# A fused attention and expert-layer kernel: the router loaded in rows on ScalarE's queue, and the hand-off from routing to the first token tiles reordered

## The chip, the cores and the metric

The kernel runs on one core of a Trainium2 chip. The metric is the device time of one execution in microseconds (us), as the median of several runs. Before the change it is 2000.14 us (three runs, 1999.53 to 2000.66).

## The reference, cut to what matters

```python
xn = layernorm(x)                       # x: 4 x 1024 x 1024, 4096 tokens in all
k, v = xn @ Wk.T + bk, xn @ Wv.T + bv
kv_sum = cumsum((elu(k) + 1) * v, axis=tokens of one sequence)
s = ((elu(xn @ Wq.T + bq) + 1) * kv_sum * SCALE) @ Wo.T + bo
logits = xn @ router_w.T                # 8 experts, the best 2 of each token
...                                     # at most 256 slots per expert, in token order
h = gelu(buf @ w1.T + b1) @ w2.T + b2   # buf: the tokens kept in their slots
g = silu(scatter(h * probs))
out = x + s * g
```

A token that no expert keeps has g = 0, so that its row of the output is x. The kernel therefore computes q, s and the expert layer only for the tokens that are kept, gathered into 2048 slots; only k, v and their running sum run over all tokens up to the last kept one.

## The kernel before, in words

**Numbers.** A product of float32 matrices is made from float16 halves: HI is the rounded value, LO the rest, and three products (HI HI, HI LO, LO HI) are added in PSUM. Making such a pair is two steps: a copy on ScalarE (`high_...`) and a scale-and-subtract on VectorE (`low_...`).

**Stage 1, the scores.** The transposed input x_t comes in 8 blocks of 512 tokens, each in two halves of 1 MB (the first half of block 0 in two quarters), on SyncE's DMA queue, behind the router's weights (line 502). TensorE starts with 11 matmuls on zeros (line 1921). Then `scores_by_expert` (line 1893) multiplies float32 x by `rw_f`, the router's weights with a ninth column of ones, 8 chunks of 128 features for each block; ScalarE copies the 9 x 512 result out (line 922), and `scores_by_token` (line 1906) turns it into rows of tokens. VectorE corrects for the mean, takes the top 2 (lines 1331 to 1345) and, behind each block, the LO halves of some of the 16 chunks of Wk and Wv (`WKV_BEHIND`: how many chunks ScalarE and VectorE split behind which block; chunks 12 to 15 are behind the last).

**Stage 2, the hand-off.** When the last block is routed, VectorE works through a chain of small operations: places of all choices within their experts (lines 1365 to 1377), which tokens are kept (1380, 1381), ranks of kept tokens (1391 to 1395), the selection matrix of tile 0 (`kept_columns`, 1399), starts of tiles and counts of loops (1405 to 1424, the signal `tables_ready`). TensorE gives it two pairs of matmuls on the way (1968/1969 and 1975/1976) and fills the time with projections of tile 0 (`project_chunks`, line 1955): half n of four is 8 chunks of 3 matmuls of 128 x 128 by 128 x 512, n = 0, 1 being k and n = 2, 3 being v, into banks 0 to 3. Then it selects: `KEPT` (line 1993) for tile 0's own kept columns, and `select_x` (line 1984) in four steps s = 0 to 3 for tile 1, each transposing half of one of HI and LO and picking the kept columns. `read_selected` (lines 492 to 497) copies both results out of PSUM, on ScalarE for s = 0, 2 and on VectorE for s = 1, 3.

**Stage 3, the token tiles.** A tile t of 128 tokens is projected while VectorE and ScalarE turn k into phi(k), multiply by v and split the product; `sum_kv` (line 2006, 16 matmuls) of the *previous* tile makes the running sums of the kept columns, and `sums` (VectorE, 1451 and 1457) adds the carry and puts them into a window that SyncE stores. Tile 0 has no previous tile: `kv_hl` and the matrix `upto[1]` are set to zero (1382, 1421) and the same code runs on zeros. ScalarE stores blocks of zeros behind the last slot (line 954). All tiles from 2 on run in a loop whose count is read from `loops_i`.

**Stage 4** is the expert layer, q and Wo, in products that are combined from sums of weights; GpSimd makes these sums (lines 784 to 812) from the moment when tile 1's k v product is split, and stores them in DRAM. It fills the time from about 500 us to the end.

**What sets the order.** Every engine has one list of instructions, written by hand, which it runs in order; semaphores tie the lists together. `stage_done` counts TensorE's transposes and selections, `stage_act` and `stage_dve` the reads of them, `wkv_ready` the chunks split, `select_ready`, `tables_ready`, `ranks_ready` and `kept_ready` the steps of the routing chain.

Of the kernel before, what the change touches and what calls it, by code (L numbers as in the profile page):

```python
# [10 lines left out]
ALU = mybir.AluOpType  # L11
# [76 lines left out]
def apart(eng):  # L88

    eng.nop(nofuse=True)  # L90


def build(nc, x, x_t, w_kv, router, w_up, w_down, b_k, b_v, b_q, b_o, b_1, b_2, out):
# [13 lines left out]
    with ExitStack() as ctx:  # L107
# [163 lines left out]
        nothing = part(16, 1)[:, 0:BLOCK // 2]  # L271
        rw_chunks = table(N4, "p (e o) -> p e o", e=EXPERTS, o=1)
# [217 lines left out]
        WKV_BEHIND = ((), (), (0,), (1, 2), (3, 4), (5, 6, 7, 8), (9, 10, 11), (12, 13, 14, 15))  # L490
# [10 lines left out]
        def _(sp):  # L501
            sp.dma_start(rw_f[:, :, 0:EXPERTS], router).then_inc(router_loaded, 16)


# [35 lines left out]
            sp.wait_ge(tables_ready, 1)  # L540
            pairs = sp.value_load(loops_i[0:1, 0:1], min_val=2, max_val=TILES // 2)
            sp.wait_ge(tables_ready, 2)
# [196 lines left out]
        def _(pool):  # L739
# [34 lines left out]

            pool.wait_ge(wkv_ready, 2 * CH)
            pool.wait_ge(tables_ready, 1)
# [130 lines left out]
        def _(act):  # L907

            def high_wkv(q):
                act.wait_ge(wkv_loaded[q % WL], 16 * (q // WL + 1))  # L910
                nc.scalar.activation(wkv[:, q, HI, :], kv_stage[q], ACT.Copy, scale=WS).then_inc(wkv_hi, 1)
# [5 lines left out]
            for b, weights in enumerate(WKV_BEHIND):  # L917
# [33 lines left out]
            with act.Fori(0, tails) as n:  # L951
                at = nc.s_assert_within(kept + n * P, 0, SLOTS)
                apart(act)
                act.dma_start(win_dram[:, :, ds(at, P)], zeros).then_inc(tail_stored, 16)
# [11 lines left out]
            def tile(t, u, first=False, second=False):  # L966
# [10 lines left out]
                at = act.value_load(start_i[0:1, ds(t + 2, 1)], min_val=0, max_val=SLOTS)  # L977
                for s in range(4) if second else (0, 2):
# [26 lines left out]

            tile(0, 0, first=True)
            tile(1, 1, second=True)
            with act.Fori(1, pairs) as g:
                for u in range(2):
                    tile(2 * g + u, u)  # L1010
# [250 lines left out]
        def _(dve):  # L1261
# [3 lines left out]
            for i, (s, n) in enumerate(((logits_read, 2), (proj_read, 4), (win_stored, 32), (tail_stored, 16),  # L1265
                         (kv_ready, 2), (stage_dve, 2))):
                nc.vector.memset(scratch[i], 0.0).then_inc(s, n)
            dve.wait_ge(router_loaded, 16)
            nc.vector.tensor_reduce(rw_chunks[:, :, :], rw_f[:, :, 0:EXPERTS].rearrange("p c e -> p e c"),
# [151 lines left out]
            nc.vector.memset(upto[1][:, :], 0.0)  # L1421
            kept_columns(1, 1)
# [18 lines left out]
            pairs = dve.value_load(loops_i[0:1, 0:1], min_val=2, max_val=TILES // 2)  # L1441
# [18 lines left out]
            def tile(t, u, g, first=False, second=False):  # L1460
# [78 lines left out]
            tile(1, 1, 0, second=True)  # L1539
            with dve.Fori(1, pairs) as g:  # L1540
# [347 lines left out]
        def _(pe):  # L1888
# [31 lines left out]
            for _ in range(11):  # L1920
                mm(out_bank(2), zeros[:, 0:P], zeros, start=True, stop=True)
            pe.wait_ge(router_loaded, 16)
# [7 lines left out]
            pe.wait_ge(zeros_ready, 2)  # L1930
            mm(bank[3][:, 0:EXPERTS], ones_f, rw_chunks[:, :, 0], start=True, stop=True).then_inc(sums_w_done, 1)
            second_half(0, 1, range(CH // 2, CH)).then_inc(scores_done, 1)
            pe.wait_ge(zeros_ready, 3)
# [15 lines left out]
            scores_by_token(1, TOKEN_BLOCKS - 1)  # L1949
# [13 lines left out]
            project_chunks(0, 0, range(CH)).then_inc(proj_done, 1)  # L1963
# [8 lines left out]
            pe.wait_ge(wkv_ready, 2 * CH)  # L1972
# [4 lines left out]
            project_chunks(0, 2, range(CH // 2, CH)).then_inc(proj_done, 1)  # L1977
# [13 lines left out]
            for h in (HI, LO):  # L1991
# [3 lines left out]
                ins.then_inc(stage_done, 1)  # L1995
# [72 lines left out]
            pe.wait_ge(tables_ready, 1)  # L2068
# [194 lines left out]
```

## Time and profile before

| | |
|---|---|
| median of three runs | 2000.14 us |
| the profiled execution, its own time | 2000.25 us |
| its span in the trace | 1998.0 us |
| TensorE busy | 1970.9 us, 99% |
| VectorE, ScalarE, GpSimd busy | 69%, 35%, 25% |
| mean granted clock of TensorE | 0.997 |

The profile lists, for each engine, groups of instructions by their line in the kernel and their start in us from the start of the span. PE is TensorE (PEld its loads of weights), DVE VectorE, ACT ScalarE, POOL GpSimd, SP SyncE; SPq, ACTq are the parts of these engines that issue DMAs. In a row of the timeline the bracket is the time for which the engine stood idle before the group, and the instruction whose end released it.

### The profile page before, as it was taken

The page shows a single profiled execution, that of the slowest core. Times are in us where ns is not written, and L with a number is a line of the kernel's source. Part 1 is how long each engine was busy: PE and PEld are TensorE (multiplying, and loading weights), DVE is VectorE, ACT ScalarE, POOL GpSimd, SP SyncE. Part 2 cuts the span into 40 slices and gives each one's busy share as a digit, 9 for nine tenths or more (in the row PEclk, how much of TensorE's full clock was granted, in tenths as well). Part 3 has the DMA queues.
Part 4 walks back from the last instruction along what each step waited for, and adds up shares of the span by engine and source line. Part 5 has one row for each costly group of instructions (what it writes and reads, how often), then busy time and mean ns, then how long its engine had stood idle before and what let it go on. Part 6 is the DMA issues. An engine that isn't in the chain of part 4 may idle for free.

```text
span 1998.0 us, 27184 instructions
## 1 busy us (share of the span) xinstructions
PE 1970.9 (99%) x9393; PEld 902.9 (45%) x9393; DVE 1378.4 (69%) x2101; ACT 707.4 (35%) x1112; POOL 504.6 (25%) x640
## 2 busy tenths in 40 slices
PE   9999999999999999999999999999999999999996
PEld 2455554455444444444444444444444444444442
DVE  4887878887877777776777797564455565456656
ACT  1432223222754344344335443522212322322322
POOL 0048888888312321321310010210000000000002
PEclk9999999999999999999999999999999999999998
DMA  9546667667999988978777879673333233335535
GB/s 388 203 141 221 228 228 236 227 212 205 304 331 286 254 243 268 281 235 279 251 263 236 293 257 324 201 222 101 102 104 101 90 114 102 111 106 159 183 114 129
DMA packets 182203, 416.26 MB, mean 208 GB/s; under 512 B 18592, under 2 KB 71376, under 8 KB 179664
## 3 DMA queue, kind: packets, MB, share of 16 engines
q1 hardware_dynamic: 138736, 284.26, 43.4%
q0 software_dynamic: 34896, 121.71, 20.0%
q10 hardware_dynamic: 8464, 8.92, 1.5%
q8 instruction: 60, 0.98, 0.2%
q14 instruction: 47, 0.39, 0.1%
HBM read 268.51 MB, written 163.10 MB: 216 GB/s over the span
## 4 chain that ended last, share of the span: by engine, by line
PE 92%; DVE 3%; DMA 2%; issue 1%; ACT 1%; SPq 0%; DVEq 0%; POOL 0%; ACTq 0%; POOLq 0%
PE pair L2145 36%; PE pair L2116 34%; PE pair L1955 16%; PE pair L1893 3%; PE pair L1984 1%; DMA arena<-up_sums 1%; PE pair L2006 1%; DMA spare<-up_sums 0%; PE pair L1906 0%; DMA arena<-x_t 0%; DVE arena L1548 0%; PE pair L2085 0%; DVE arena L1321 0%; DVE root L1300 0%; DVE arena L1315 0%
## 5 line engine op out<-in xcount | busy, mean ns | idle before, releaser
L2145 PE MATMUL pair<-arena 128*128 128x512 f16 x3360 | 730.2, 379 | 1.1 <-DVE arena L1694 0.5
L2116 PE MATMUL pair<-xnT,arena 128*128 128x512 f16 x2400 | 525.4, 379 | 2.1 <-ACT xnT L1044 1.9
L2145 PEld LDWEIGHTS pair<-arena 128*128 128x128 f16 x3360 | 327.8, 98 | 400.2 <-issue 7.2
L1686 DVE SCALAR_TENSOR_TENSOR arena<-pair,arena 128x1024 f32<-128x1024 f32 x234 | 286.0, 1223 | 150.7 <-PE pair L2145 149.8
L1955 PE MATMUL pair<-arena 128*128 128x512 f16 x1728 | 382.9, 379 | 1.7 <-DVE xnT L497 1.0
L1118 ACT ACTIVATE arena<-arena 128x512 f16<-128x512 f32 x280 | 171.4, 626 | 554.8 <-PE pair L2145 500.0
L2116 PEld LDWEIGHTS pair<-xnT,arena 128*128 128x128 f16 x2400 | 234.4, 98 | 286.6 <-ACT xnT L1044 3.4
L1955 PEld LDWEIGHTS pair<-arena 128*128 128x128 f16 x1728 | 168.6, 98 | 194.1 <-issue 1.9
L2116 PE MATMUL pair<-xnT 128*128 128x512 f16 x960 | 213.7, 379 | 0.0
L1661 DVE SCALAR_TENSOR_TENSOR arena<-arena 128x512 f16<-128x512 f32 x280 | 189.3, 688 | 16.4 <-ACT arena L1118 15.7
L839 POOL DMA_DIRECT2D s_dram<-arena x8 | 6.2, 776 | 596.4 <-DVE arena L1686 596.4
L1044 ACT ACTIVATE xnT<-pair 128x512 f32<-128x512 f32 x120 | 71.2, 594 | 220.2 <-PE pair L2116 220.1
L2116 PEld LDWEIGHTS pair<-xnT 128*128 128x128 f16 x960 | 93.9, 98 | 113.3
L858 POOL DMA_INDIRECT meta_dram<-meta,slot_i x32 | 33.5, 1048 | 367.0 <-PE pair L2145 304.7
L1567 DVE SCALAR_TENSOR_TENSOR arena<-arena 128x1024 f16<-128x1024 f32 x70 | 85.5, 1223 | 27.6 <-ACT arena L1037 27.1
L1105 ACT ACTIVATE arena<-arena,b_c 128x512 f32<-128x512 f32 x96 | 69.2, 721 | 74.7 <-DVE arena L1597 39.1
L972 ACT ACTIVATE arena<-arena 128x512 f32<-128x512 f32 x36 | 22.7, 629 | 162.4 <-DVE arena L1465 162.4
L1604 DVE TENSOR_TENSOR arena<-xnT,pair 128x512 f32<-128x512 f32 x40 | 27.4, 686 | 74.2 <-PE pair L2116 74.0
L1561 DVE SCALAR_TENSOR_TENSOR arena<-arena 128x512 f16<-128x512 f32 x82 | 59.0, 720 | 21.5 <-ACT arena L1026 20.0
L1037 ACT ACTIVATE arena<-arena 128x1024 f16<-128x1024 f32 x70 | 72.8, 1043 | 0.0
L1608 DVE TENSOR_TENSOR arena<-xnT,pair 128x512 f32<-128x512 f32 x40 | 27.5, 687 | 62.7 <-ACT xnT L1044 62.7
L1597 DVE TENSOR_TENSOR arena<-xnT,pair 128x512 f32<-128x512 f32 x40 | 27.4, 685 | 54.4 <-PE pair L2116 53.9
(217 smaller groups left out, 1817.5 us busy)
## 6 DMA issues: line engine op xcount, KB each, us to landing
down_dram<-arena SPq DMA_DIRECT2D x70, 512.0 KB, 7.0
arena<-down_dram SPq DMA_DIRECT2D x70, 512.0 KB, 3.3
up_dram<-arena SPq DMA_DIRECT2D x90, 256.0 KB, 6.0
arena<-up_dram SPq DMA_DIRECT2D x90, 256.0 KB, 2.6
arena<-down_sums SPq DMA_DIRECT2D x40, 512.0 KB, 6.1
arena<-w_up POOLq DMA_DIRECT2D x36, 512.0 KB
up_sums<-arena POOLq DMA_DIRECT2D x36, 512.0 KB, 3.8
arena<-up_sums SPq DMA_DIRECT2D x66, 256.0 KB, 6.1
```

What stands on the lines that cost most here:

```text
L1037: nc.scalar.activation(down_ring[:, j, :, HI, :], down_stage[d % DS].rearrange("p (c n) -> p c n", c=2), ACT.Copy, scale=WM).then_inc(down ...
L1044: nc.scalar.activation(dst, in_rows(src), ACT.Copy).then_inc(copy_ready, 1)
L1105: nc.scalar.activation(g_block(name), src, ACT.Gelu, bias=b1_c[:, col:col + 1], scale=INV_XM)\
L1118: nc.scalar.activation(g_ops[:, A_NAMES.index(name), k % 2, HI, :], g_block(name), ACT.Copy, scale=CS if is_attention(n) else HS).then_inc ...
L1561: nc.vector.scalar_tensor_tensor(up_ring(j)[:, LO, :], up_stage[a % US], WM, up_ring(j)[:, HI, :], ALU.mult, ALU.subtract).then_inc(up_w[j ...
L1567: nc.vector.scalar_tensor_tensor(down_ring[:, j, :, LO, :], down_stage[d % DS].rearrange("p (c n) -> p c n", c=2), WM, down_ring[:, j, :, ...
L1661: nc.vector.scalar_tensor_tensor(to[:, LO, :], g_block(name), CS if is_attention(k // 2) else HS, to[:, HI, :], ALU.mult, ALU.subtract).th ...
L1686: ins = nc.vector.scalar_tensor_tensor(to, src, scale, to, ALU.mult, ALU.add)
L1893: ins = mm(scores(u), rw_f[:, c, :], xt_in[u][:, c, :], start=(c == 0), stop=(c == CH - 1))
L1955: ins = mm(out_bank(n), xT[u][:, a, c, :], wkv[:, (n // 2) * CH + c, b, e], start=(c == 0 and i == 0), stop=(c == CH - 1 and i == 2), skip ...
L2116: ins = mm(out_to, w[:, a, c * P:(c + 1) * P], x_in_op[:, b, c, :], start=(first and i == 0), stop=(i == 11), skip_group_check=True)
L2145: ins = mm(down_banks(j, t // 2)[:, (t % 2) * BLOCK:(t % 2 + 1) * BLOCK], g_ops[:, A_NAMES.index(DOWN_A[j]), c, a, t * P:(t + 1) * P], dow ...
```

## The change

The router's weights are loaded contiguously into a scratch table `rw_in`, from ScalarE's queue, and VectorE copies them into `rw_f`; SyncE's first DMA is now x_t. TensorE runs 8 matmuls on zeros, not 11. The three matmuls of the first chunk of projection 0 stand ahead of the last `scores_by_token`. VectorE splits chunks 14 and 15 behind `kept_ready`, not ahead of the places; both selection matrices are made one after the other; two subtractions for the softmax move behind them and raise `tables_ready` by one, on which ScalarE now reads `KEPT`. For tile 0, `sum_kv` and `sums` are gone; GpSimd sets `kv_hl` and window 0 to zero. TensorE's `select_x` steps for tile 1 and the projection chunks between them are dealt out anew, and ScalarE reads step 0 ahead of its stores of zeros.

```diff
-        WKV_BEHIND = ((), (), (0,), (1, 2), (3, 4), (5, 6, 7, 8), (9, 10, 11), (12, 13, 14, 15))
+        WKV_BEHIND = ((), (), (0,), (1, 2), (3, 4), (5, 6, 7, 8), (9, 10, 11), (12, 13))
+        WKV_LAST = (14, 15)
 @block.sync
-            sp.dma_start(rw_f[:, :, 0:EXPERTS], router).then_inc(router_loaded, 16)
 @block.gpsimd
+            pool.wait_ge(scores_done, TOKEN_BLOCKS)
+            nc.gpsimd.memset(kv_hl[:, :, :], 0.0).then_inc(kvlo_ready, 2)
+            pool.wait_ge(wkv_ready, 12)
+            nc.gpsimd.memset(window[0], 0.0).then_inc(win_ready, 1)
 @block.scalar
+            act.dma_start(rw_in, router).then_inc(router_loaded, 16)
...
+            for q in WKV_LAST:
+                high_wkv(q)
+            act.wait_ge(wkv_ready, SOON)
             act.wait_ge(tables_ready, 1)
-            act.wait_ge(wkv_ready, SOON)
             for h in (HI, LO):
                 act.wait_ge(stage_done, 3 + h)
                 ins = copy(xnT[:, h, :, 0:P], all_chunks(KEPT[h]))
             ins.then_inc(stage_act, 1)
-            pairs = act.value_load(loops_i[0:1, 0:1], min_val=2, max_val=TILES // 2)
             act.wait_ge(tables_ready, 2)
+            at = act.value_load(start_i[0:1, 2:3], min_val=0, max_val=SLOTS)
+            act.wait_ge(stage_done, 6)
+            apart(act)
+            read_selected(copy, 1, 0, 3, ds(at, P), stage_act)
+            act.wait_ge(tables_ready, 3)
...
 @block.vector
+            nc.vector.tensor_copy(rw_f[:, :, 0:EXPERTS], rw_in).then_inc(zeros_ready, 1)
...
             nc.vector.tensor_copy(kept_h[:, :], kept).then_inc(kept_ready, 1)
-            nc.vector.memset(kv_hl[:, :, :], 0.0).then_inc(kvlo_ready, 2)
-            for k in range(TOPK):
-                nc.vector.tensor_tensor(prob[:, k, :], top_v[:, :, k], top_v[:, :, 0], ALU.subtract)
-            nc.vector.tensor_tensor(logits[:, :, :], logits[:, :, :],
-                                    top_v[:, :, 0:1].to_broadcast((P, TILES, EXPERTS)), ALU.subtract)
+            for q in WKV_LAST:
+                low_wkv(q)
             dve.wait_ge(ranks_ready, 1)
...
-            kept_columns(0, 0).then_inc(select_ready, 1)
+            for u in range(2):
+                kept_columns(u, u).then_inc(select_ready, 1)
             nc.vector.tensor_tensor_scan(run_kept, run_mask[:, 0, :], tile_kept, 0.0, ALU.mult, ALU.add)
+            for k in range(TOPK):
+                nc.vector.tensor_tensor(prob[:, k, :], top_v[:, :, k], top_v[:, :, 0], ALU.subtract)
+            nc.vector.tensor_tensor(logits[:, :, :], logits[:, :, :],
+                                    top_v[:, :, 0:1].to_broadcast((P, TILES, EXPERTS)), ALU.subtract).then_inc(tables_ready, 1)
...
-            nc.vector.memset(upto[1][:, :], 0.0)
-            kept_columns(1, 1)
...
-                read_k(0)
+                if not first:
+                    read_k(0)
-                sums(u, t, 5 * t + 4)
+                if not first:
+                    sums(u, t, 5 * t + 4)
                 if first:
                     read_odd(1)
+                    read_k(0)
+                    read_odd(3)
                     read_k(1)
-                    read_odd(3)
 @block.tensor
-            for _ in range(11):
+            for _ in range(8):
...
-            scores_by_token(1, TOKEN_BLOCKS - 1)
...
-            project_chunks(0, 0, range(CH)).then_inc(proj_done, 1)
+            project_chunks(0, 0, range(1))
+            scores_by_token(1, TOKEN_BLOCKS - 1)
+            project_chunks(0, 0, range(1, CH)).then_inc(proj_done, 1)
...
-            project_chunks(0, 2, range(CH // 2, CH)).then_inc(proj_done, 1)
+            pe.wait_ge(wkv_ready, WKV_LAST[0])
+            project_chunks(0, 2, range(CH // 2, CH - 2))
+            pe.wait_ge(wkv_ready, 2 * CH)
+            project_chunks(0, 2, range(CH - 2, CH)).then_inc(proj_done, 1)
...
             project_chunks(0, 3, range(0, 3))
             pe.wait_ge(stage_act, 2)
-            pe.wait_ge(kvlo_ready, 2)
-            sum_kv(0, 1, 4)
+            pe.wait_ge(select_ready, 2)
             pe.wait_ge(kxlo_ready, 2)
             select_x(1, 0, 3)
+            select_x(1, 1, 2)
             project_chunks(0, 3, range(3, 5))
-            pe.wait_ge(stage_dve, 3)
-            select_x(1, 1, 2)
-            project_chunks(0, 3, range(5, 7))
             pe.wait_ge(stage_act, 3)
             select_x(1, 2, 3)
+            project_chunks(0, 3, range(5, 6))
             pe.wait_ge(stage_dve, 4)
             select_x(1, 3, 2)
-            project_chunks(0, 3, range(7, CH)).then_inc(proj_done, 1)
+            project_chunks(0, 3, range(6, CH)).then_inc(proj_done, 1)
```

The counts of `stage_done`, `stage_dve` and `tables_ready` that the removed steps raised are raised elsewhere, and loop counts are read later on ScalarE, VectorE and TensorE.

## Rows read from the trace of the kernel before

**Rows 1.** The page, part 1: busy time of each engine.
```profile
PE 1970.9 (99%) x9393; PEld 902.9 (45%) x9393; DVE 1378.4 (69%) x2101; ACT 707.4 (35%) x1112; POOL 504.6 (25%) x640
```

**Rows 2.** The waits of TensorE over the whole span: us in total, times, longest.
```profile
PE pair L2116 <- ACT xnT L1044: 1.9, 3, 1.1
...
PE pair L1955 <- DVE xnT L497: 1.0, 2, 0.6
```

**Rows 3.** The timeline from 0 to 17 us: start, us, engine and line.
```profile
0.80 0.68 SPq L502 DMA_DIRECT2D rw_f<-router  x1
...
1.26 4.40 PE L1921 MATMUL pair<-arena 128*128 128x512 f16 x11 [1.26 <-DVE arena L1263]
...
1.43 0.52 POOL L749 MEMSET xnT<- 128x512 f32 x1
...
1.54 0.63 SPq L517 DMA_DIRECT2D arena<-x_t  x1
...
5.63 3.59 PE L1893 MATMUL pair<-arena,rw_f 128*9 128x512 f32 x8
...
10.20 5.32 PE L1893 MATMUL pair<-arena,rw_f 128*9 128x512 f32 x12 [0.65 <-DMA arena<-x_t]
```

**Rows 4.** Line 1921 alone, up to 5.2 us: durations in ns, min/median/max.
```profile
L1921 PE MATMUL pair<-arena x10: 380/634/634, 1.3 to 5.1; 128*128 128x512 f16 x10
```

**Rows 5.** DMAs: issues with KB and us to landing; one from the chain of waits.
```profile
arena<-x_t SPq DMA_DIRECT2D x1, 512.0 KB, 4.0
rw_f<-router SPq DMA_DIRECT2D x1, 32.0 KB, 3.1
...
2.69 7.46 DMA arena<-x_t
```

**Rows 6.** Busy time from 15 to 30 us; last: granted clock, DMA share, GB/s.
```profile
15.00:30.00 15.00, 15.00 (x48) 4.50 (x47) 6.29 (x44) 0.85 (x2) 0.00 (x0) 1.00 1.03 421
```

**Rows 7.** The timeline of TensorE from 60 to 112 us.
```profile
71.21 1.05 PE L1906 MATMUL pair<-xnT 9*128 9x9 f32 x8 [0.68 <-ACT xnT L922]
...
86.02 0.19 PE L1975 MATMUL pair<-kept_h,xnT 128*128 128x32 f16 x1 [0.27 <-DVE kept_h L1381]
...
92.28 1.07 PE L2006 MATMUL pair<-spare,arena 128*128 128x128 f16 x16 [0.62 <-ACT xnT L915]
...
99.11 10.52 PE L1955 MATMUL pair<-arena 128*128 128x512 f16 x48 [0.78 <-ACT xnT L915]
109.47 1.06 PE L2006 MATMUL pair<-spare,arena 128*128 128x128 f16 x16
```

**Rows 8.** The chain that ended last: tile 1's `sum_kv` as a piece of it.
```profile
109.63 0.89 PE pair L2006 x16
```

**Rows 9.** The timeline of VectorE from 74 to 106 us.
```profile
74.49 4.62 DVE L1321 SCALAR_TENSOR_TENSOR arena<-arena 128x1024 f16<-128x1024 f32 x4
...
85.78 0.18 DVE L1381 CAST kept_h<-routing 128x32 f16<-128x32 f32 x1
86.11 0.91 DVE L1382 MEMSET arena<- 128x1024 uint32 x1 [0.16 <-issue]
...
88.20 0.29 DVE L1399 TENSOR_SCALAR spare<-spare,rank_kept 128x128 f16<-128x128 f32 x1
...
92.75 0.69 DVE L1465 SCALAR_TENSOR_TENSOR arena<-pair,arena 128x512 f32<-128x512 f32 x1 [0.82 <-issue]
...
98.33 0.68 DVE L497 CAST xnT<-pair 128x512 f32 x1
...
103.80 1.47 DVE L1528 SCALAR_TENSOR_TENSOR arena<-arena 128x512 f16<-128x512 f32 x2
```

**Rows 10.** The timeline of ScalarE from 60 to 125 us.
```profile
90.29 1.94 ACT L915 ACTIVATE xnT<-pair 128x1024 f16<-128x1024 f32 x2 [15.35 <-DVE routing L1424]
92.59 0.46 ACTq L954 DMA_DIRECT2D kvs_dram<-arena  x1
94.18 0.60 ACT L915 ACTIVATE arena<-pair 128x512 f16<-128x512 f32 x1 [1.96 <-PE pair L1984]
```

More of the change, by code:

```diff
@@ L271, in build @@
         nothing = part(16, 1)[:, 0:BLOCK // 2]
+        rw_in = table(0, "p (c e) -> p c e", c=CH, e=EXPERTS)
         rw_chunks = table(N4, "p (e o) -> p e o", e=EXPERTS, o=1)
@@ L537, in _ @@
             sp.dma_start(b1_c[:, :], b_1).then_inc(biases_loaded, 16)
-            sp.wait_ge(tables_ready, 1)
+            sp.wait_ge(tables_ready, 2)
             pairs = sp.value_load(loops_i[0:1, 0:1], min_val=2, max_val=TILES // 2)
-            sp.wait_ge(tables_ready, 2)
+            sp.wait_ge(tables_ready, 3)
             tails = sp.value_load(loops_i[0:1, 1:2], min_val=1, max_val=SLOT_TILES + 1)
@@ L951, in _ @@
             with act.Fori(0, tails) as n:
-                at = nc.s_assert_within(kept + n * P, 0, SLOTS)
+                at_n = nc.s_assert_within(kept + n * P, 0, SLOTS)
                 apart(act)
-                act.dma_start(win_dram[:, :, ds(at, P)], zeros).then_inc(tail_stored, 16)
+                act.dma_start(win_dram[:, :, ds(at_n, P)], zeros).then_inc(tail_stored, 16)
             def zero_columns():
@@ L964, in zero_columns, with tile @@
                 act.wait_ge(x_filled, 1)
-            def tile(t, u, first=False, second=False):
+            def tile(t, u, start=None, first=False, second=False):
                 def exp_k(half):
@@ L976, in tile @@
                     exp_k(0)
-                at = act.value_load(start_i[0:1, ds(t + 2, 1)], min_val=0, max_val=SLOTS)
-                for s in range(4) if second else (0, 2):
+                if first:
+                    act.wait_ge(stage_done, 8)
+                    apart(act)
+                    read_selected(copy, 1, 2, 3, ds(start, P), stage_act)
+                else:
+                    at = act.value_load(start_i[0:1, ds(t + 2, 1)], min_val=0, max_val=SLOTS)
+                for s in () if first else range(4) if second else (0, 2):
                     act.wait_ge(stage_done, 5 * t + 4 + 1 + s + 1)
@@ L1004, in tile @@
                     high_x()
-            tile(0, 0, first=True)
+            tile(0, 0, at, first=True)
             tile(1, 1, second=True)
+            pairs = act.value_load(loops_i[0:1, 0:1], min_val=2, max_val=TILES // 2)
             with act.Fori(1, pairs) as g:
@@ L1265, in _ @@
             for i, (s, n) in enumerate(((logits_read, 2), (proj_read, 4), (win_stored, 32), (tail_stored, 16),
-                         (kv_ready, 2), (stage_dve, 2))):
+                         (kv_ready, 2), (stage_dve, 3))):
                 nc.vector.memset(scratch[i], 0.0).then_inc(s, n)
             dve.wait_ge(router_loaded, 16)
-            nc.vector.tensor_reduce(rw_chunks[:, :, :], rw_f[:, :, 0:EXPERTS].rearrange("p c e -> p e c"),
+            nc.vector.tensor_copy(rw_f[:, :, 0:EXPERTS], rw_in).then_inc(zeros_ready, 1)
+            nc.vector.tensor_reduce(rw_chunks[:, :, :], rw_in.rearrange("p c e -> p e c"),
                                     AX.X, ALU.add).then_inc(zeros_ready, 1)
@@ L1440, in _ @@
             dve.wait_ge(rows_loaded, 16)
-            pairs = dve.value_load(loops_i[0:1, 0:1], min_val=2, max_val=TILES // 2)
             def sums(u, t, n):
@@ L1539, in _ @@
             tile(1, 1, 0, second=True)
+            pairs = dve.value_load(loops_i[0:1, 0:1], min_val=2, max_val=TILES // 2)
             with dve.Fori(1, pairs) as g:
@@ L1919, in _ @@
             zeros = nothing.bitcast(F16)
-            for _ in range(11):
+            for _ in range(8):
                 mm(out_bank(2), zeros[:, 0:P], zeros, start=True, stop=True)
-            pe.wait_ge(router_loaded, 16)
+            pe.wait_ge(zeros_ready, 2)
             pe.wait_ge(pool_consts, 1)
@@ L1928, in _ @@
             pe.wait_ge(pool_consts, 2)
-            pe.wait_ge(zeros_ready, 2)
+            pe.wait_ge(zeros_ready, 3)
             mm(bank[3][:, 0:EXPERTS], ones_f, rw_chunks[:, :, 0], start=True, stop=True).then_inc(sums_w_done, 1)
             second_half(0, 1, range(CH // 2, CH)).then_inc(scores_done, 1)
-            pe.wait_ge(zeros_ready, 3)
+            pe.wait_ge(zeros_ready, 4)
             with pe.Fori(0, TOKEN_BLOCKS // 2 - 1) as g:
@@ L1971, in _ @@
             project_chunks(0, 1, range(CH)).then_inc(proj_done, 1)
-            pe.wait_ge(wkv_ready, 2 * CH)
+            pe.wait_ge(wkv_ready, CH + CH // 2)
             project_chunks(0, 2, range(CH // 2))
@@ L1994, in _ @@
                              start=True, stop=True)
-                ins.then_inc(stage_done, 1)
+                ins.then_inc(stage_done, 2 if h == LO else 1)
             def project(u, t, n):
@@ L2067, in _ @@
             project_chunks(1, 3, range(CH // 2, CH)).then_inc(proj_done, 1)
-            pe.wait_ge(tables_ready, 1)
+            pe.wait_ge(tables_ready, 2)
             pairs = pe.value_load(loops_i[0:1, 0:1], min_val=2, max_val=TILES // 2)
```

2 lines of the change are left out of this document (1 added, 1 removed).

## The prediction

> **What bounds the kernel now.** I read the busy times first: TensorE works for 1970.9 of 1998.0 us [rows 1], so only two things can shorten the run: work taken from TensorE, or its gaps. The waits over the whole span come next. The longest entries outside the stretch that the change touches are 1.9 and 1.0 us [rows 2]; the rest of the idle time lies in the first 100 us, before the loop over tiles. So I took the timeline of that stretch. TensorE stands idle until 1.26 us, 0.65 us at 10.20 for x_t [rows 3], and then in the hand-off 0.68, 0.27, 0.62 and 0.78 us, together 2.35 [rows 7]. The rows model the end of a matmul, some 0.16 us past the moment when the next may start, so counted from start to start these four gaps are worth about 2.85 us. The reader should see in [rows 7] who ends each: ScalarE's copy of the last scores, VectorE's `kept_h`, and ScalarE and VectorE reading the selections.
>
> **The start.** The router's DMA takes SyncE from 0.80 us; the first x_t is issued at 1.54 us [rows 3] and lands 4.0 us later, the router 3.1 us after its issue; the second half of block 0 takes 7.46 us from 2.69 and lands at 10.15 [rows 5], which ends TensorE's gap at 10.20. Without the router's issue all x_t issues move up by 1.54 - 0.80 = 0.74 us, and that landing comes at 9.4. Is TensorE ready for it? Eight zero matmuls at 0.43 us each (their start to start, as 4.40 us for 11 gives) end at 1.26 + 3.4 = 4.7; the first x_t lands at 0.80 + 4.0 = 4.8, the router at 0.80 + 3.1 = 3.9 with some 0.3 for VectorE's new copy. From the first real matmul to the gap TensorE had 9.55 - 5.63 = 3.9 us of work, so it is ready at 8.8 and x_t decides: gain 0.75 us. Behind it the DMA engines are full, share 1.03 at 421 GB/s [rows 6], while TensorE never waits, so stream and scores move up together. Bounds: nothing, if the stream doesn't come sooner; 1.1 us, if the many small packets of the old router load also held up the first x_t.
>
> The clock: the granted clock reads 1.00 in the windows, but the zero matmuls have a median of 634 ns and only the last show 380 [rows 4], so the engine was at 1.2 GHz of its 2.4 until about 5.1 us, after close to 4 us of matmuls. The new kernel starts real matmuls at 4.8, a little before; at half speed up to 5.1 they lose 0.15 us, which the 0.6 us between 8.8 and 9.4 covers. The Trainium skill, "TensorE: Matmul & The Clock Gate", section "What's actually happening", says that the throttled state is the default and that activity releases it, at a moment that varies from run to run. By that rule three fewer zero matmuls are no loss if real ones follow at once, and a loss if TensorE then waits; the trace has no such gap to show it.
>
> The Trainium skill, "DMA: Bandwidth & Descriptors", section "Queues, rings and completion order", speaks against the other half: SP and ACT have a ring each on the same 16 DMA engines, which alternate between them. Then the router no longer goes ahead of x_t but shares with it and lands later. From the rows above, TensorE may begin as late as 9.4 - 3.9 = 5.5 us without losing anything, so the router may come 1.3 us later than 3.9. Nothing in the sum changes.
>
> **The hand-off, step by step, on the old clock.** Prices: a 128x512 projection matmul 10.52/48 = 0.22 us; `sum_kv` 0.89 us [rows 8]; one `low_wkv` 4.62/4 = 1.15 us; ScalarE's two reads of `KEPT` 1.94 us [rows 10].
> - *First chunk ahead of the last scores by token.* Three matmuls, 0.65 us, fill the gap of 0.68 before 71.21 [rows 7]; what they wait for (ScalarE's transposed copies) is done by 70.3. The scores by token don't start later. The remaining 21 matmuls end at 76.7, the places' matmuls at 77.2.
> - *Two splits behind the chain.* VectorE had four splits, 74.49 to 79.1, then the places, and `kept_h` done at 85.96 [rows 9]. With two it is free at 76.8, and TensorE decides at 77.4: `kept_h` at 84.3, 1.65 us earlier. TensorE reaches it after 36 matmuls, at 84.95: the gap of 0.27 is gone.
> - *The splits now stand where VectorE waited on ranks.* Two of them, 84.3 to 86.6, against the memset of 0.91 us and two subtractions before [rows 9]; so the ranks are read at 86.6 instead of 87.44, and the selection matrix is done at 87.65 instead of 88.49. TensorE has six matmuls until 86.3, waits 0.3 us for chunk 15, and is at `KEPT` at 87.9: the selection is ready, no wait.
> - *ScalarE reads `KEPT` on the first signal.* It waited for the loop counts until 90.29 [rows 10]. Now the signal comes after the second matrix, a scan and the subtractions, 0.9 us after 87.65, at 88.55; 1.94 us later is 90.55. TensorE, with `KEPT` done at 88.8 and nine matmuls, arrives at 90.75: the gap of 0.62 is gone.
> - *No sums of zeros.* 0.89 us of TensorE vanish. VectorE loses `sums`, 1.6 us. GpSimd's two memsets are 1.04 us each, twice the 0.52 of half the size [rows 3], at about 71 us while it has nothing else; that hides them.
> - *The four selections.* Steps 0 and 1 follow at once, 90.75 to 91.6; six matmuls to 92.9. ScalarE reads step 0 from 91.45, done 92.6; no wait. Step 2 to 93.35, three matmuls to 94.0. VectorE comes out of its tables at 91.6; a load of a register and a start took 0.82 us before 92.75 [rows 9], so step 1 is read from 92.4 to 93.7: no wait, by 0.3 us. Step 3 to 94.45, six matmuls to 95.75. VectorE reads it in 1.3 us (the old last cast starts at 98.33, ends 99.01 and frees TensorE at 99.11), so until 96.0; ScalarE's read of step 2 waits behind its register loads and store of zeros, which took at most 94.18 - 92.23 = 1.95 us [rows 10]: 94.5 to 95.6.
>
> TensorE starts tile 1's projections at 96.05 instead of 99.11: **3.06 us**, that is 0.89 of work and 2.85 of gaps less 0.7 of new ones. Bounds: 3.74 with no new gap; 2.0 if the margins of 0.15 to 0.3 us all turn into waits of half a microsecond.
>
> **Does it last?** `sum_kv` of tile 0 is needed 10.4 us later; its halves were ready at 105.27 for 109.47 [rows 7, 9]. The one thing that doesn't move up is the store of zeros, issued at 92.6 to 92.95 as before, for which ScalarE's split of tile 0 waits; it landed 7.4 us after its issue, so the halves are ready about 102.8 for 106.4. GpSimd's sums start on tile 1's halves and move up too. The sum is 0.75 + 3.06 = 3.8 us. Against the profiled execution's 2000.25 us, 0.1 above the median, that is 1996.45, and 1996.4 against the median.
>
> **Rivals.**
> 1. *Only the hand-off pays* (0.14): the stream of x_t, full already [rows 6], or a late clock takes the start. 2000.1 - 3.1 = 1997.0.
> 2. *The fills turn into waits* (0.12): VectorE's step 1 and step 3 reads come late because its tables end late. Then the selections gain 1.0 us less and more: 0.75 + 2.2 = 2.9 to 2.0, 1997.7.
> 3. *Later waits go too* (0.08): the 2.9 us of [rows 2] depend on moments of other queues; with 1 us of them gone, 1995.3.
> 4. *The gain is swallowed* (0.06): if something that doesn't move up paces the expert layer, as the sums of weights could. For it: the waits at line 2116. Against: they start on tile 1. 2000.
> 5. *Slower: the low clock stays* (0.03). If the clock doesn't rise at 5.1 but TensorE's pause at 9 us keeps it low, matmuls at 1.2 GHz lose half their time. It costs nothing up to 0.6 us, and eats the whole 3.8 when it lasts 8.8 us, to 13.6; lasting to 20 us it costs 7.3, so 2003.
>
> The forecast keeps 0.57.
>
> **The numbers.** A measurement of this kernel tells about 0.2% from no change, 4.0 us; the forecast's gain of 3.8 lies just under it. Of the forecast's cases two fifths or more pass 4.0 (the start's upper bound, gaps fully closed), with rival 3 and a little of the first: faster 0.42, within 0.2% 0.54, slower 0.04. The range takes a gain of 4.9 (1.1 + 3.74) down to 2.0: 1995.2 to 1998.1.
>
> **What would show it.** The changed profile should have x_t issued at 0.8; the group of 12 of line 1893 at about 9.45; scores by token without a gap; `kept_h` 2.4 us earlier than 85.78 with the start's share in it; no line 2006 before tile 1's projections; these at 95.3, with gaps of some 0.3 us at chunk 15 and in front of them; and the rest 3.8 us earlier. A gap of over 0.5 us at any selection, or the 12 still at 10.2, would make it wrong.

## The result, and the profile after

Thirteen executions of each give 1996.25 us for the changed kernel (1994.4 to 1997.97) against 2000.26 us (1998.34 to 2001.91): a ratio of 0.9982 with a 95% interval of 0.9975 to 0.9989, so 3.6 us faster by the ratio (2000 us times 0.0018), between 2.2 and 5.0; the two medians are 4.0 us apart. A second set of eleven, below, gave 0.9989 (0.998 to 0.9998), which is 2.2 us. The kernel is faster, by about 0.15% over both, which lies within the 0.2% that the forecast held likelier, if not by much.

The page of the changed kernel, its busy times:

```profile
PE 1968.0 (99%) x9374; PEld 902.0 (45%) x9374; DVE 1381.7 (69%) x2097; ACT 706.4 (35%) x1112; POOL 512.9 (26%) x642
```

TensorE has 2.9 us less of busy time than in [rows 1] and 19 matmuls fewer: 3 on zeros at the start and 16 of tile 0's sum.

The start, in the timeline from 0 to 12 us (compare [rows 3]):

```profile
0.81 0.40 SPq L516 DMA_DIRECT2D arena<-x_t  x1
0.81 0.41 ACTq L913 DMA_DIRECT2D xnT<-router  x1
...
1.26 3.25 PE L1942 MATMUL pair<-arena 128*128 128x512 f16 x8 [1.26 <-DVE arena L1281]
...
4.83 0.21 DVE L1287 COPY rw_f<-xnT 128x64 f32<-128x64 f32 x1 [3.58 <-DMA xnT<-router]
...
5.10 3.60 PE L1914 MATMUL pair<-arena,rw_f 128*9 128x512 f32 x8 [0.59 <-DVE rw_f L1287]
...
8.95 3.60 PE L1914 MATMUL pair<-arena,rw_f 128*9 128x512 f32 x8
```

and the landing of the DMAs issued in the first 2 us (KB, us from issue to landing; compare [rows 5]):

```profile
arena<-x_t SPq DMA_DIRECT2D x2, 512.0 KB, 4.2
arena<-x_t SPq DMA_DIRECT2D x1, 1024.0 KB, 6.6
xnT<-router ACTq DMA_DIRECT2D x1, 32.0 KB, 4.0
```

x_t is issued at 0.81, as forecast. But its late half, issued at 1.73, lands 6.6 us later, at 8.3 and not at 9.4, so that no gap is left in front of block 0's second group of matmuls: it starts at 8.95, when TensorE is ready, 1.25 us earlier than at 10.20. (6.6 us is the shortest of all executions; the others, below, say what of it is the change.) What now decides the start is the router: it lands 4.0 us after its issue instead of 3.1, and VectorE's copy comes on top.

The hand-off, in TensorE's timeline (compare [rows 7]):

```profile
69.22 0.82 PE L1975 MATMUL pair<-arena 128*128 128x512 f16 x3
69.97 1.05 PE L1927 MATMUL pair<-xnT 9*128 9x9 f32 x8
...
83.70 0.18 PE L1997 MATMUL pair<-kept_h,xnT 128*128 128x32 f16 x1
...
85.38 1.47 PE L1975 MATMUL pair<-arena 128*128 128x512 f16 x6 [0.17 <-DVE arena L1340]
86.69 1.06 PE L2018 MATMUL pair<-spare,arena 128*128 128x128 f16 x16
87.58 2.10 PE L1975 MATMUL pair<-arena 128*128 128x512 f16 x9
89.52 1.04 PE L2009 MATMUL pair<-spare,arena 128*128 128x256 f16 x8
...
93.21 12.11 PE L1975 MATMUL pair<-arena 128*128 128x512 f16 x54
105.16 1.06 PE L2032 MATMUL pair<-spare,arena 128*128 128x128 f16 x16
```

One gap is left that the rows show, in front of chunk 15. A second hides inside the group of 54: at 0.216 us each, plus the 0.16 us of the last one's end, it would take 11.8 us, and it takes 12.11. The missing 0.3 us are the wait for VectorE's read of the fourth selection, whose two casts end at 94.70:

```profile
93.41 0.69 DVE L498 CAST arena<-pair 128x512 f16<-128x512 f32 x1 [0.40 <-PE pair L2009]
94.02 0.68 DVE L499 CAST xnT<-pair 128x512 f32 x1
```

Counted back from 105.16, 48 matmuls at 0.216 us start at 94.8; ScalarE had read its part by 93.9. Tile 1's sum of k v starts at 105.16 instead of 109.47, 4.31 us earlier.

Yet the span is only 2.8 us shorter. The waits of TensorE over the whole span show where some of it went (us in total, times, longest; compare [rows 2]):

```profile
PE pair L2139 <- DVE xnT L1569: 1.9, 1, 1.9
...
PE pair L2139 <- ACT xnT L1062: 1.1, 1, 1.1
PE pair L2108 <- DVE routing L1577: 1.1, 1, 1.1
PE pair L2108 <- DVE arena L1569: 0.8, 1, 0.8
```

All four lie between 500 and 551 us, at the head of stage 4. They sum to 4.9 us, against 2.0 in the profile of before. Three questions follow: what made the start better than forecast, is the hand-off what the steps said, and is the loss at 500 us part of the change?

For all runs I use three marks in TensorE's timeline: A, the start of block 0's second group; B, the start of tile 1's sum of k v; and the waits between 490 and 600 us.

### The profile page after: what moved, and what is told of

Read it like the earlier page. It is cut to its first block, busy times and chain, and to the rows that moved or that the text cites. A ratio compares the mean times of both kernels' runs of the same rounds, so it can differ in the third digit from the quotient of the medians.

```text
span 1995.2 us, 27144 instructions
## 1 busy us (share of the span) xinstructions
PE 1968.0 (99%) x9374; PEld 902.0 (45%) x9374; DVE 1381.7 (69%) x2097; ACT 706.4 (35%) x1112; POOL 512.9 (26%) x642
## 3 DMA queue, kind: packets, MB, share of 16 engines
q10 hardware_dynamic: 8608, 8.95, 1.5%
## 4 chain that ended last, share of the span: by engine, by line
PE 94%; DVE 2%; DMA 1%; issue 1%; ACT 1%; SPq 0%; POOL 0%; ACTq 0%; DVEq 0%; POOLq 0%
PE pair L2168 36%; PE pair L2139 34%; PE pair L1975 18%; PE pair L1914 3%; PE pair L2009 2%; PE pair L2032 1%; PE pair L2108 1%; PE pair L1927 0%; DMA spare<-up_sums 0%; DMA routing<-kvs_dram 0%; DVE arena L1569 0%; DVE arena L1682 0%; DMA xnT<-router 0%; DVE arena L1588 0%; ACT arena L1118 0%
```

## The experiments

**1. The start alone.** On the kernel before:

```diff
-            sp.dma_start(rw_f[:, :, 0:EXPERTS], router).then_inc(router_loaded, 16)
+            act.dma_start(rw_in, router).then_inc(router_loaded, 16)
...
+            nc.vector.tensor_copy(rw_f[:, :, 0:EXPERTS], rw_in).then_inc(zeros_ready, 1)
...
-            for _ in range(11):
+            for _ in range(8):
...
```

> The kernel before with the start's edits alone: router in rows from ScalarE's queue, a copy by VectorE, 8 matmuls on zeros. Theory (the parts add up: 1.24 us at the start, 3.06 us in the hand-off): tile 1's sum of k v starts 1.2 us before the 109.47 us of the kernel before, at 108.2, with the four gaps of the hand-off as they were (2.35 us), and the whole is faster by 0.6 to 1.8 us. Rival (the scores are faster only because the hand-off's list is different): 109.4 and no gain. Second rival (the late part of the kernel swallows what comes early): 108.2 there, but the end not earlier.

A at 9.27, B at 108.55: 0.92 us earlier than before, with the four gaps of the hand-off as they were. B - A is 99.28 us, against 99.27 before. A came 0.3 us later than the expectation had it. The whole: 2000.26 us against 2000.41, ratio 0.9998 (0.9989 to 1.0007): 0.4 us by the ratio, under the 0.6 expected, with an interval that holds the 0.9 us and also nothing. The profiled execution of this run has waits of 5.1 us at 490 to 600 us. That speaks for the second rival as far as one execution goes; runs 8, 9, 11 and 12 take this up.

**2. The hand-off alone.** The changed kernel with the router from SyncE's queue in small pieces and 11 matmuls on zeros.

> The changed kernel with the old start: router in small pieces from SyncE's queue, 11 matmuls on zeros. Theory: tile 1's sum of k v starts at 109.47 - 3.06 = 106.4 us, the first real matmul at 5.6, the gap of 0.65 at 10.20 back; the whole is faster than before by 2.5 to 3.7 us. Rival (late part swallows): 106.4 there, but under 1.5 us at the end.

A at 10.47, B at 106.68. B - A is 96.21 us, exactly as in the changed kernel (105.16 - 8.95). So the hand-off is worth 99.27 - 96.21 = 3.06 us. The absolute place is 0.3 us later than expected, all of it ahead of A. The expected gap at A is not back: the 11 matmuls on zeros took 4.87 us and not 4.40, the eight real ones 4.17 and not 3.59, so that x_t, landed at 9.5, was there before TensorE was ready. The whole: 0.9991 (0.9982 to 1.0), 1.8 us faster by the ratio, under the 2.5 expected, with an interval that reaches 3.6.

**3. Small pieces from ScalarE's queue.** The changed kernel with this edit, and without the copy:

```diff
-            act.dma_start(rw_in, router).then_inc(router_loaded, 16)
+            act.dma_start(rw_f[:, :, 0:EXPERTS], router).then_inc(router_loaded, 16)
...
```

> The changed kernel with the router still in 1024 pieces of 32 bytes, but from ScalarE's queue, and no copy by VectorE. It tells position in the queue from size of the pieces. Theory (the small pieces take the DMA engines for some 0.9 us, whatever queue they come from): the late half of block 0 lands near 9.4 us, not 8.3, and TensorE has a gap in front of it; its second group of block 0 starts at 9.4 to 9.6, against 8.95 in the changed kernel. Rival (only the place of SyncE's issue counts): it lands by 8.5 and the group starts at 8.95.

For A neither held. The chain of waits up to 30 us:

```profile
0.81 13.39 DMA rw_f<-router
14.20 0.04 issue
14.24 5.82 PE pair L1913 x8
20.06 0.32 PE pair L1951 x2
20.38 5.25 PE pair L1913 x12
```

The router took 13.4 us to land, and TensorE stood idle for 9.4 us. The time of this execution is 2011.6 us. The packets tell what happened, first from 3.5 to 4 us, then from 6 to 14 us, with the queues (q1 is SyncE's, q10 ScalarE's):

```profile
DMA packets 535, 0.13 MB, mean 253 GB/s; under 512 B 508, under 2 KB 508, under 8 KB 535
```

```profile
q1 hardware_dynamic: 469, 3.18, 97.8%
...
q10 hardware_dynamic: 91, 0.00, 0.6%
```

About half of the 1024 pieces passed within half a microsecond, but 91 were still going between 6 and 14 us, while SyncE's queue moved 3.18 MB. The rule that I cited of the Trainium skill's page "DMA: Bandwidth & Descriptors", section "Queues, rings and completion order" (two queues share the 16 DMA engines and alternate), agrees with this in part: packets of both queues pass side by side. It doesn't by itself account for the tail, in which 469 packets of SyncE's queue passed beside 91 of the router's; why these were so late is not shown. The same 32 KB as 128 rows landed in 4.0 us. So in this start the two halves of the edit belong together: ScalarE's queue is only usable because the router comes in rows. My expectation, that x_t's late half would suffer, can't be read from A, since the router hid it, but it can be read from the landing, issued at 1.73:

```profile
arena<-x_t SPq DMA_DIRECT2D x1, 1024.0 KB, 7.8
```

It landed at 9.5, near the 9.4 of the theory; with rows the same transfer takes 6.6 to 7.7 us. The second of the two quarters ahead of it took 5.5 us against 4.6 to 4.8. So in this execution the small pieces beside x_t cost the stream 0.7 to 0.9 us there, and at least 0.1 at the late half. The run shows something else on the way: in the windows the granted clock fell in the idle stretch (last three numbers: granted clock, DMA share, GB/s), and the eight matmuls behind it took 5.82 us instead of 3.60.

```profile
6.00:14.00 8.00, 0.00 (x0) 0.00 (x0) 0.00 (x0) 0.00 (x0) 0.00 (x0) 0.66 0.99 400
```

**4. Rows from SyncE's queue, ahead of x_t.**

```diff
-            act.dma_start(rw_in, router).then_inc(router_loaded, 16)
+            sp.dma_start(rw_in, router).then_inc(router_loaded, 16)
```

> The changed kernel with the router in rows, but from SyncE's queue ahead of x_t. Theory: the router lands sooner, near 3.5 us, and x_t's issues all come 0.45 us later, so that the first x_t decides: first real matmul at 5.5 instead of 5.10, second group of block 0 at 9.35 instead of 8.95, with no gap in front of it. Rival (the issue's place is worth the 0.74 us that it took before): first real matmul 5.8, second group 9.7.

The chain of waits up to 12 us:

```profile
0.81 0.40 SPq L504
1.21 0.05 issue
1.26 3.78 DMA arena<-x_t
5.04 0.14 issue
5.18 4.25 PE pair L1914 x8
9.43 0.32 PE pair L1952 x2
```

The issue takes 0.40 us, x_t comes 0.45 us later and lands at 5.04; the first real matmul is at 5.18, 0.08 us behind the changed kernel, and so earlier than both the theory's 5.5 and the rival's 5.8. The late half was issued at 2.20 and landed at 9.0. A is at 9.68, but only because the eight matmuls took 4.25 us instead of 3.60; with these 0.65 us off it would be 9.03. That it stands near the rival's 9.7 is the clock, then, and not the place of the issue. So with rows the queue matters little. It also splits what the old load cost: in the kernel before the late half is issued at 2.69, in the changed one at 1.73, here at 2.20. Of the 0.96 us a load ahead of x_t takes 0.47, and its 1024 pieces another 0.49, since SyncE needs 0.68 us for their issue and not 0.40, and 0.63 for the next one and not 0.42. The packets from 2.5 to 3 us, first the kernel before, then the changed one:

```profile
DMA packets 701, 0.05 MB, mean 93 GB/s; under 512 B 695, under 2 KB 695, under 8 KB 701
```

```profile
DMA packets 58, 0.14 MB, mean 275 GB/s; under 512 B 26, under 2 KB 26, under 8 KB 58
```

In that half microsecond the kernel before moved 695 small pieces and 0.05 MB, the changed one 0.14 MB, nearly all of it x_t. But there x_t had also been issued 0.73 us earlier, so these rows alone don't say what the pieces took from it.

**5. The sum of zeros put back.**

```diff
+            for c in range(CH):
+                for h in (HI, LO):
+                    mm(bank[2][:, c * P:(c + 1) * P], kv_hl[:, h, c * P:(c + 1) * P], select[0][:, 1, :],
+                       start=(h == HI), stop=(h == LO))
...
```

> The changed kernel with 16 matmuls of 128 columns on the zeroed half sums put back in front of the selections for tile 1; nobody reads their result. Theory (TensorE is the bound there and its gaps are nearly closed): tile 1's sum of k v starts 0.6 to 0.9 us later than the 105.16 us of the changed kernel, at 105.8 to 106.05, since the gap of 0.3 us in front of tile 1's projections can give some back only if VectorE isn't later too. Rival (VectorE's and ScalarE's reads of the selections set the pace): 105.2.

A 9.01, B 106.12, just beyond the 106.05 expected. B - A is 97.11, 0.90 us more: the full price of 16 matmuls, none of it absorbed.

**6. Chunks 14 and 15 split ahead of the places.**

```diff
-        WKV_BEHIND = ((), (), (0,), (1, 2), (3, 4), (5, 6, 7, 8), (9, 10, 11), (12, 13))
-        WKV_LAST = (14, 15)
+        WKV_BEHIND = ((), (), (0,), (1, 2), (3, 4), (5, 6, 7, 8), (9, 10, 11), (12, 13, 14, 15))
+        WKV_LAST = ()
...
```

> The changed kernel with chunks 14 and 15 split by VectorE ahead of the places, as before. Theory: the places start at 78.0 instead of 76.13, kept_h is ready 1.8 us later than 83.0, TensorE gets a gap of 1.0 to 1.4 us in front of the matmuls of kept_h (reached at 83.70 before), but ranks and tables are then read with nothing in between: select 0.4 us or less later. Tile 1's sum of k v at 105.9 to 106.4. Rival (the rest of the list has room for it): a gap of that size, made good by the gap at chunk 15 and by later ones, 105.4 or less.

The gap is back, in TensorE's timeline:

```profile
85.59 0.19 PE L1997 MATMUL pair<-kept_h,xnT 128*128 128x32 f16 x1 [0.90 <-DVE kept_h L1400]
```

The gap of 0.90 us is under the 1.0 to 1.4 expected. B at 106.72, beyond the range, because A came at 9.78; B - A is 96.94, 0.73 us more than 96.21, which the theory had as 0.7 to 1.2. So the splits' move is worth 0.73 us.

**7. The first chunk behind the last scores.**

```diff
-            project_chunks(0, 0, range(1))
             scores_by_token(1, TOKEN_BLOCKS - 1)
-            project_chunks(0, 0, range(1, CH)).then_inc(proj_done, 1)
+            project_chunks(0, 0, range(CH)).then_inc(proj_done, 1)
```

> The changed kernel with the first chunk of projection 0 behind the last scores by token, as before. Theory: the gap of 0.65 us in front of them comes back, places and everything behind move by 0.65: tile 1's sum of k v at 105.8. Rival (VectorE has room ahead of the places, so only TensorE's later gaps shrink): under 0.3 us, 105.4.

```profile
70.17 1.02 PE L1927 MATMUL pair<-xnT 9*128 9x9 f32 x8 [0.88 <-ACT xnT L928]
```

A 8.95, B 105.98, B - A 97.03: 0.82 us more, of which 0.65 are the three matmuls. The other 0.2 us are already in the row: the scores by token start at 70.17 and not at 69.97, although ScalarE's copy starts at the same 69.33 to 0.01 us. Why is open.

**8. The changed kernel again.**

> The changed kernel once more, for a second profile. It asks whether the waits of 1.06, 0.78, 1.87 and 1.11 us at 501 to 551 us are a price of the change. Theory (these depend on moments of the DMA queues and differ from execution to execution): their sum differs by over 1 us from the first profile's 4.8. Rival (stage 4's head doesn't move up with the tiles): they sum to 4.3 to 5.3 again. Tile 1's sum of k v at 105.2 within 0.2 in either case.

A 9.12, B 105.33, B - A 96.21. The waits at 490 to 600 us sum to 4.3 us: that is inside the rival's range and not a microsecond away from 4.9, so this run speaks for the rival. Run 11 has 3.0 and speaks for the theory.

**9 and 12. The kernel before, twice.**

> The kernel before once more, for a second profile. From the second group of block 0 to tile 1's sum of k v the first profile has 109.47 - 10.20 = 99.27 us. Theory (that stretch is fixed, everything else varies between executions): 99.27 within 0.05, but the waits between 300 and 600 us sum to something else than 1.0 + 0.7 + 1.3 = 3.0 us, by up to 2 us. Rival (the kernel before has shorter waits at the head of stage 4 than the changed one's 4.3 to 4.9): 2.0 there again.

> The kernel before, third profile: as for the second. If the waits at 490 to 600 us are 2.0 within 0.5 in all three, the changed kernel pays there for coming early; if one is over 3.5, it does not.

B - A is 99.30 and 99.27. The waits at 490 to 600 us are 2.6 and 3.5 us, against 2.0 in the first profile: they are neither all within 0.5 of 2.0 nor is one clearly over 3.5, so by the terms of the expectation the question stays open here.

**11. The changed kernel, timed again.**

> The changed kernel beside the one above, on the same chip: 3.6 to 4.3 us faster than the kernel before. Theory: the stretch from block 0's second group to tile 1's sum is 96.21 us again, and what lies ahead of it differs by up to 0.9 us with the moment at which the clock rises. Rival (the start is fixed too): 8.95 for block 0's second group.

A 8.98, B 105.19, B - A 96.21. The waits at 490 to 600 us are 3.0 us here. The whole: 1997.65 us against 2000.18, ratio 0.9989 (0.998 to 0.9998), 2.2 us by the ratio, less than the 3.6 expected, with an interval from 0.4 to 4.0. A came close to the rival's 8.95, but 9.12 in run 8 and more in other runs speak for the theory.

**10. One split behind, and the last selection sooner.** A version aimed at the two gaps that were left:

```diff
-        WKV_BEHIND = ((), (), (0,), (1, 2), (3, 4), (5, 6, 7, 8), (9, 10, 11), (12, 13))
-        WKV_LAST = (14, 15)
+        WKV_BEHIND = ((), (), (0,), (1, 2), (3, 4), (5, 6, 7, 8), (9, 10, 11), (12, 13, 14))
+        WKV_LAST = (15,)
...
-            project_chunks(0, 2, range(CH // 2, CH - 2))
+            project_chunks(0, 2, range(CH // 2, CH - 1))
...
-            project_chunks(0, 3, range(5, 6))
             pe.wait_ge(stage_dve, 4)
             select_x(1, 3, 2)
-            project_chunks(0, 3, range(6, CH)).then_inc(proj_done, 1)
+            project_chunks(0, 3, range(5, CH)).then_inc(proj_done, 1)
```

> The changed kernel with only chunk 15 split behind kept_h (chunk 14 ahead of the places again, where VectorE stood idle for 0.53 us), and chunk 5 of the last projection moved behind the last selection. It aims at the two gaps that are left in the hand-off, 0.17 and 0.3 us. Theory: kept_h 0.6 us later and just in time, ranks 0.5 us earlier; from block 0's second group to tile 1's sum 95.75 to 95.85 us, against 96.21. Rival (one of the two margins is too thin): one gap moves to kept_h or to the last selection, 96.1 or more. The whole against the kernel before: 3.4 to 4.9 us faster.

```profile
84.54 0.18 PE L1997 MATMUL pair<-kept_h,xnT 128*128 128x32 f16 x1
...
93.16 12.47 PE L1975 MATMUL pair<-arena 128*128 128x512 f16 x57
105.46 1.06 PE L2032 MATMUL pair<-spare,arena 128*128 128x128 f16 x16
```

No row of the hand-off has a gap any more, and 57 matmuls take 12.47 us, which is 57 at 0.216 and the last one's end. B - A is 105.46 - 9.79 = 95.67 us, 0.54 less than in the changed kernel and a little under the 95.75 expected. The whole: 1995.59 us against 2000.18, ratio 0.9978 (0.9969 to 0.9987), 4.4 us, as expected. Its interval overlaps with that of the changed kernel in the same series (0.998 to 0.9998), so as a whole it is the fastest kernel by its median, and better for certain only in the stretch B - A.

The marks of all runs in one table (us; the last column is the sum of TensorE's waits between 490 and 600 us; in run 3 the stretch in front of B has no comparable A):

| run | A | B | B - A | waits |
|---|---|---|---|---|
| before: first profile, 9, 12 | 10.20, 10.21, 10.11 | 109.47, 109.51, 109.38 | 99.27, 99.30, 99.27 | 2.0, 2.6, 3.5 |
| changed: first profile, 8, 11 | 8.95, 9.12, 8.98 | 105.16, 105.33, 105.19 | 96.21 in all three | 4.9, 4.3, 3.0 |
| 1, start alone | 9.27 | 108.55 | 99.28 | 5.1 |
| 2, hand-off alone | 10.47 | 106.68 | 96.21 | 3.0 |
| 3, small pieces | - | 116.53 | - | 4.1 |
| 4, rows from SyncE | 9.68 | 105.90 | 96.22 | 4.5 |
| 5, sum of zeros back | 9.01 | 106.12 | 97.11 | 3.2 |
| 6, splits ahead | 9.78 | 106.72 | 96.94 | 5.0 |
| 7, chunk behind | 8.95 | 105.98 | 97.03 | 4.1 |
| 10, one split behind | 9.79 | 105.46 | 95.67 | 2.5 |

## Why the prediction was right, and which of its steps were not

**The sum.** Forecast were 3.8 us and 1996.4 us; measured were 1996.25 us in the first series, 1997.65 in the second. The range held both. By the ratios the gain was 3.6 and 2.2 us, so the forecast's 3.8 lies above both and inside both intervals. That it came so near is in part luck: the lines of the sum did not all come out. The start was worth more than its line, and part of the gain at B did not reach the end in the first profiles.

**The hand-off: right.** 3.06 us were forecast and 3.06 measured, by two pairs of kernels, each alike in the start and different in the hand-off, or the other way round, that agree to 0.01 us. Its parts, each undone by itself: sum of zeros 0.90 (0.89 forecast), first chunk 0.82 (0.65), two splits 0.73. Together these are 2.45 us. Parts undone singly need not add up to the whole, and the rest, the earlier signal for `KEPT` and the new order of the selections, no run undid by itself; the rows show that the gap of 0.62 us is gone and the one of 0.78 down to 0.3. That the total agrees to the hundredth is luck in so far as a single part was off by 0.17. The step that `kept_h` comes 1.65 us earlier is confirmed: VectorE's cast starts at 82.88 instead of 85.78 [rows 9], 2.90 us, of which 1.25 are the start's. The new gap in front of chunk 15 was forecast as 0.3 us counted from start to start and is 0.17 as the rows count, which is the same; the second, 0.3 us in front of tile 1, is there. No margin of 0.15 to 0.3 us tipped over, so rival 2 did not happen. Two figures beside the sum were off and changed nothing in it: the four gaps with 0.16 us more each are 2.99 and not 2.85 us (the 3.06 comes from the two starts, 99.11 and 96.05), and in rival 5 half of the 15.2 us from 4.8 to 20, less 0.6, is 7.0 and not 7.3.

**The start: the mechanism half right, the term mis-sized.** The step that failed is "x_t decides: gain 0.75 us". It had two errors. First, x_t's late half moves up by more than SyncE's first issue: it is issued at 1.73 and not at 2.69, 0.96 us earlier and not 0.74, since the issue behind the small pieces was slower too. Second, I took 10.15 as the landing of the kernel before, and 9.4 behind it, but the landing varies. With the old start (first profile, runs 9, 12, 2) it is 10.15, 9.7, 10.1 and 9.5, on average 9.85; with the new one (first profile, runs 1, 5, 6, 7, 8, 10, 11) it is 8.3 to 9.4, on average 8.8. From issue to landing that is 6.8 to 7.5 us with the old start and 6.6 to 7.7 with the new: no difference that stands out. So nearly all of the 1.1 us on average is the issue; that the pieces ahead of x_t cost its transfer anything more, as the first pair of profiles (7.46 against 6.6) seems to say, is not shown.

What decides A is therefore TensorE itself in every execution with the new start, none of which has a gap in front of A, and in two of the four with the old one. The price at the other end was not seen either: the router lands 4.0 to 4.2 us after its issue, not 2.6 to 3.1, and is now what TensorE's first real matmul waits for, at 5.10 to 5.27. How much of the gain at A comes from the three zero matmuls fewer, and how much from the router, no run separates.

**The clock: costlier than forecast.** I gave 0.15 us for real matmuls at the low clock and said that a gap of 0.6 would cover it. The gap doesn't exist any more, and the moment of the rise differs between executions: by the durations of single matmuls it came at about 4.1 us in the first profile of the changed kernel (a matmul on zeros started at 3.8 took 494 ns, the next 380) and at about 6.8 in run 10 (a real one started at 5.9 took 1047 ns, the next 623). The eight real matmuls of block 0's first half took 3.60 us in the first profile of the changed kernel, and 4.44 in run 10, 4.37 in run 6, 4.25 in run 4, 3.79 in run 1. In the other four with this start it was 3.60 again. That moves A by up to 0.84 us, from 8.95 to 9.79, and through it all that follows. The prediction had fewer zeros as a loss if TensorE then waits; the runs don't show that: behind waits of 0.59 and 0.76 us (first profile, run 8) the eight took 3.60, and behind 0.24 and 0.31 (runs 10 and 6) 4.44 and 4.37. The rows of run 10:

```profile
1.26 3.60 PE L1942 MATMUL pair<-arena 128*128 128x512 f16 x8 [1.26 <-DVE arena L1281]
5.10 4.44 PE L1914 MATMUL pair<-arena,rw_f 128*9 128x512 f32 x8 [0.24 <-DVE rw_f L1287]
```

In the kernel before the same lateness is partly hidden by the wait for x_t. In run 9 the 11 zeros took 4.87 us and the eight 3.90, and A was still 10.21: TensorE had used up the gap of 0.65 us and set A itself, since x_t had landed at 9.7:

```profile
1.26 4.87 PE L1921 MATMUL pair<-arena 128*128 128x512 f16 x11 [1.26 <-DVE arena L1263]
6.06 3.90 PE L1893 MATMUL pair<-arena,rw_f 128*9 128x512 f32 x8
9.89 0.39 PE L1931 MATMUL pair<-xnT 128*128 128x8 f32 x2
10.21 5.32 PE L1893 MATMUL pair<-arena,rw_f 128*9 128x512 f32 x12
```

Over the eight executions with the new start A is 9.23 on average, over the four with the old one 10.25: the start is worth 1.0 us on average, and against the first profile's 10.20 between 0.4 and 1.25. The rule that the moment varies, on the Trainium skill's page "TensorE: Matmul & The Clock Gate", section "What's actually happening", is what these rows show, though they differ by more than the 500 ns either way that the page gives.

**"Does it last?": only in part.** The stretch up to B is 4.23 us shorter on the average of three profiles each. The last piece of the chain of waits, GpSimd's last scatter, begins at 1984.82, 1984.36 and 1984.44 in the kernel before, at 1981.32, 1981.73 and 1980.24 in the changed one: 3.4 us on average. About 0.8 us are lost between. The changed kernel's waits at the head of stage 4 average 4.1 us, the other's 2.7. But run 2, with the same hand-off, has 3.0, and run 1, with the old one, has 5.1, so it doesn't go with the hand-off; run 3, whose tiles come 11 us later, has 4.1, so it doesn't go with the time of arrival either.

One rival is left, the start. From B to that last piece the executions of all kernels take 1874.5 to 1878.4 us, a spread as large as the gain, but the four with the old start are all among the short ones, 1874.5 to 1875.4, with waits of 2.8 us on average; those with the new start take 1874.6 to 1878.4, with waits of 4.1. It would fit run 1, whose 0.9 us at B can't be seen in the whole time. Against it, the four profiles taken on one and the same chip show no loss: 1874.85 and 1875.06 in runs 9 and 12 with the old start, 1875.05 and 1874.58 in runs 11 and 10 with the new. No row shows how the start could reach so far. Whether 0.8 us of the gain are paid back there as a rule, because of the start, or are chance, is open; it would take many profiles of each.

## What to carry to other kernels

In a chain where one engine is the bound, price every gap by who ends it, and write the whole new list with times before making the change: here that gave the 3.06 us measured, since the order is fixed and the margins were counted. Look at the size of a DMA's pieces before its queue: here 1024 pieces of 32 bytes ahead of a stream put off its issue by 0.96 us and 128 rows by 0.47; on another queue beside it the pieces landed after 13.4 us, the rows after 4.0. And take a landing time from several profiles: that of the kernel before varied by 0.7 us, as much as the term that was built on it. And for gains of 0.2% read fixed marks in the trace, because the whole time varies by as much from execution to execution.

## What the hardware did that I had not expected

- The same 32 KB landed 2.6 to 3.1 us after issue as 1024 pieces ahead of x_t in the same queue, 13.4 us as 1024 pieces in ScalarE's queue beside it, 4.0 to 4.2 us as 128 rows beside it, and 1.8 us as 128 rows ahead of it (the second and the last in one execution each).
- TensorE's clock rose at different moments in executions of kernels with the same first 5 us: with 8 matmuls on zeros from 1.26 us, the group behind them took 3.60 to 4.44 us, while the granted clock of the windows read 1.00 all along.
- By the profile's spans GpSimd's memset of 128 x 2048 float16 took 1.80 us, that of 128 x 1024 float32, the same bytes, 0.95 us. I had put both at 1.04. It had nothing else to do.

```profile
69.42 1.80 POOL L776 MEMSET arena<- 128x2048 f16 x1 [64.37 <-PE pair L1914]
71.16 0.95 POOL L778 MEMSET arena<- 128x1024 f32 x1
```
